# Perceiver block, context projection: values laid out in memory by chunk, partition and head, last chunk's values computed sooner, its writes waited for in the next stage

## What is computed

```python
q = (x @ Wq).reshape(B, N, HEADS, hd).transpose(0, 2, 1, 3)
k = (context @ Wk).reshape(B, M, HEADS, hd).transpose(0, 2, 1, 3)
v = (context @ Wv).reshape(B, M, HEADS, hd).transpose(0, 2, 1, 3)
scores = jnp.einsum('bhid,bhjd->bhij', q, k) * scale
scores = jnp.where(context_mask[:, None, None, :], scores, max_neg)
attn = jax.nn.softmax(scores, axis=-1)
```

## Time and profile before

| | us |
|---|---|
| median of three runs | 3372.61 |
| the profiled execution | 3372.62 |
| its span in the trace | 3370.9 |
| PE busy | 2945.2 (87%) |
| DVE busy | 1830.0 (54%) |
| ACT busy | 1350.9 (40%) |
| POOL busy | 404.1 (12%) |

### The profile page before, as it was taken

One profiled execution on the slowest core, in us unless ns is written; L12 is line 12 of the kernel. 1 busy time (PEld: TensorE's weight loads), 2 busy tenths in 40 slices (PEclk: granted clock), 3 DMA queues, 4 the chain that ended last, 5 costly groups with the idle time before them and its releaser, 6 DMA issues. The chain is left out here.

```text
span 3370.9 us, 66496 instructions
## 1 busy us (share of the span) xinstructions
PE 2945.2 (87%) x27158; PEld 2487.7 (74%) x27158; DVE 1830.0 (54%) x3246; ACT 1350.9 (40%) x2191; POOL 404.1 (12%) x571
## 2 busy tenths in 40 slices
PE   6999809998768999477999669999999999999978
PEld 6888706776564777463777455999999999999867
DVE  5555418774527775446776343555555555555524
ACT  4444305665003666123667120444444444444311
POOL 2443400000100000000000002220202020200000
PEclk9999958998787999686999685999999999999969
DMA  4898879882468883158884271100101010000016
GB/s 154 281 289 270 269 152 182 177 176 64 153 187 177 174 176 78 46 191 178 175 176 101 82 220 36 52 18 22 39 1 39 1 39 1 1 1 1 17 50 227
DMA packets 251093, 393.95 MB, mean 117 GB/s; under 512 B 45827, under 2 KB 214149, under 8 KB 250789
## 3 DMA queue, kind: packets, MB, share of 16 engines
q1 hardware_dynamic: 250791, 389.70, 45.3%
HBM read 289.45 MB, written 99.49 MB: 115 GB/s over the span
## 5 line engine op out<-in xcount | busy, mean ns | idle before, releaser
L712 DVE TENSOR_REDUCE L_xattn_tops<-psum 128x1 f32<-128x896 f32 x672 | 702.4, 1086 | 270.3 <-PE psum L564 269.1
L625 ACT ACTIVATE L_xattn_probs<-psum 128x512 f32<-128x512 f32 x1176 | 612.3, 600 | 518.2 <-PE psum L575 518.1
L1720 DVE TENSOR_TENSOR L_units_low<-psum,L_units_high 128x896 fp32r<-128x896 f32 x224 | 243.6, 1088 | 486.8 <-ACT L_units_high L1669 486.8
L564 PE MATMUL psum<-L_xattn_keys,L_xattn_q_stack 96*128 96x448 bf16 (+1 forms) x1344 | 395.2, 378 | 110.5 <-DMA L_xattn_q_stack<-query_parts 65.2
L1637 PE MATMUL psum<-wide_tokens,L_units_high 128*128 128x386 f32 x1568 | 456.5, 358 | 1.4 <-DVE L_units_low L1720 1.4
L575 PEld LDWEIGHTS psum<-L_xattn_q_stack,L_xattn_keys 99*128 99x128 bf16 (+1 forms) x4704 | 323.1, 98 | 144.4 <-issue 19.2
L575 PE MATMUL psum<-L_xattn_q_stack,L_xattn_keys 99*128 99x128 bf16 (+1 forms) x4704 | 394.2, 221 | 5.0 <-ACT L_xattn_probs L625 5.0
L1638 PE MATMUL psum<-wide_tokens,L_units_low 128*128 128x194 f32 x1568 | 395.1, 252 | 0.0
L588 PE MATMUL psum<-L_xattn_probs,L_xattn_values 128*17 128x128 f32 x9408 | 358.5, 277 | 0.2 <-issue 0.2
L1669 ACT CAST L_units_high<-psum 128x896 fp32r<-128x896 f32 x224 | 203.3, 908 | 363.7 <-PE psum L1625 363.7
L1661 ACT ACTIVATE L_units_raw<-L_units_raw,L_units_negmax 128x896 f32<-128x896 f32 x224 | 221.6, 1036 | 308.4 <-DVE L_units_negmax L1711 308.4
(11 more groups left out here) (436 smaller groups left out, 3990.6 us busy)
## 6 DMA issues: line engine op xcount, KB each, us to landing
key_parts<-proj_parts SPq DMA_DIRECT2D x84, 672.0 KB, 5.1
L_xattn_keys<-key_parts SPq DMA_DIRECT2D x144, 336.0 KB, 4.7
values_scratch<-proj_values SPq DMA_DIRECT2D x18, 1904.0 KB, 11.9
L_xattn_values<-values_scratch SPq DMA_DIRECT2D x144, 238.0 KB, 5.4
L_ffn_w<-in_L_ffn_W SPq DMA_DIRECT2D x32, 1024.0 KB, 6.8
L_xattn_keys<-key_parts SPq DMA_DIRECT2D x144, 224.0 KB, 5.0
L_xattn_keys<-key_parts SPq DMA_DIRECT2D x192, 112.0 KB, 5.1
L_ffn_w<-in_L_ffn_w SPq DMA_DIRECT2D x16, 1024.0 KB, 6.3
```

The lines of the kernel that those rows point to most:

```text
L564: last = pe.matmul(top_slot(n)[:, s, :], q_stack[0:P1, h, :], keys[0:P1, v % RING, key:key + WIN // 2], start=True, stop=True)
L625: act.activation(group_probs(k), score_bank(k), ACT.Exp).then_inc(sem("probs"), 1)
L712: dve.tensor_reduce(tops[:, h % 2, 2 * c + w:2 * c + w + 1], top_slot(n), AX.XY, ALU.max)\
L1720: dve.tensor_tensor(low[gr][:], turned_banks(gr), high[gr][:], ALU.subtract).then_inc(sem("low"), 1)
```

## The change

- **Layout.** `g.values` is (layer, chunk, partition, head, 14 x 17) instead of (layer, head, chunk, partition, 14 x 17). A write of a layer's chunk is 128 runs of 15232 bytes. A load of one head's values still reads runs of 952 bytes, now 15232 bytes apart instead of one behind the other.
- **Last two halves.** Their order is written out as `LAST`: 12 key tiles, with two value tiles behind each of the first seven. PE waits for both halves' `split` ahead of it. The last chunk goes out in three whole writes at key tiles 7, 8 and 9 of the twelve, the chunk before it at tiles 0, 2 and 4.
- **Waits.** The projection no longer waits for its writes. Their semaphores outlive the stage; the next one's SP waits for them after the load of the query weights and ahead of the rows of ones. There `keys`, `values` and `probs` are allocated last.
- **Beginning.** SP loads context half 0 first, then the six `w_a` tiles, half 1, and writes the mask row. ACT issues the mask's load, the twelve `w_b` loads and the four biases. Half 0 is rounded and split ahead of the weights.
- **Mask.** The work on the mask (DVE, one matmul, the write of the row) is moved from layer 0's cross-attention to the projection's beginning.

```diff
+        late = [("value", i, t) for i in (NH - 2, NH - 1) for t in range(GT)]
+        LAST = []
+        for i in (NH - 2, NH - 1):
+            for n in range(NK2):
+                LAST.append(("key", i, n))
+                LAST.extend(late[:2])
+                del late[:2]
...
             def store_values(c, l):
                 sp.wait_ge(sem("values"), TPC * (c + 1))
-                dst = dram(g.values, l * g.layer_values + c * 128 * TPC * VW,
-                           [[TPC * VW, 128], [NCH * 128 * TPC * VW, H], [1, TPC * VW]])
-                src = values[c % 2][:, l * H:l * H + H, :, :].rearrange("p h t e -> p h (t e)")
-                sp.dma_start(dst, src).then_inc(sem(f"values_out{c % 2}"), 16)
...
+                dst = dram(g.values, l * g.layer_values + c * 128 * H * TPC * VW,
+                           [[H * TPC * VW, 128], [1, H * TPC * VW]])
+                src = values[c % 2][:, l * H:l * H + H, :, :].rearrange("p h t e -> p (h t e)")
+                sp.dma_start(dst, src).then_inc(written(f"values_out{c % 2}"), 16)
...
+            load(0)
             for l in range(NL):
                 cols = slice(l * D, l * D + D)
                 for w, name in ((0, "Wk"), (1, "Wv")):
...
+                    sp.dma_start(w_a[:, w, cols], a[f"L{l}_xattn_{name}"][0:128, :]).then_inc(sem("weights"), 16)
             load(1)
-            for i in range(NH):
+            sp.wait_ge(sem("drop"), 1)
+            sp.dma_start(dram(g.mask_row, 0, [[NK // 128, 128], [1, NK // 128]]), drop_bf[:])\
+              .then_inc(written("mask_out"), 16)
+            for i in range(NH - 2):
                 for n in range(NK2):
...
-            for l in range(NL):
-                store_last(1, l)
-            for r in range(RING):
-                sp.wait_ge(sem(f"parts_out{r}"), 16 * len(range(r, NH * NK2, RING)))
-            for r in range(2):
-                sp.wait_ge(sem(f"values_out{r}"), 16 * NL * (len(range(r, NCH, 2)) + (r == (NCH - 1) % 2)))
+            for n in range(2 * NK2):
+                store_parts((NH - 2) * NK2 + n)
+                if n in (0, 2, 4):
+                    store_values(NCH - 2, n // 2)
+                if n in (7, 8, 9):
+                    store_values(NCH - 1, n - 7)
...
+            pe.wait_ge(sem("some"), 1)
+            pe.matmul(bank(g, 7, 0, 1), g.ones[:], some[:], start=True, stop=True).then_inc(sem("mask_count"), 1)
             pe.wait_ge(sem("weight_parts"), 4)
-            for i in range(NH):
+            pe.wait_ge(sem("drop"), 1)
+            for i in range(NH - 2):
...
+            pe.wait_ge(sem("split"), 2 * NH)
+            for kind, i, n in LAST:
+                (key_tile if kind == "key" else value_tile)(i, n)
...
+            act.dma_start(mask8[:], a["mask"].rearrange("(p n) -> p n", p=128)).then_inc(sem("mask"), 16)
+            for l in range(NL):
...
+                        act.dma_start(w_b[copy * C1:copy * C1 + C1, w, cols], a[f"L{l}_xattn_{name}"][128:C, :])\
+                           .then_inc(sem("weights"), 16)
...
+            round_context(0)
             act.wait_ge(sem("weights"), LOADS)
             act.copy(wh_a[:], w_a[:]).then_inc(sem("weights_rounded"), 1)
             act.copy(wh_b[:], w_b[:]).then_inc(sem("weights_rounded"), 1)
-            round_context(0)
             round_context(1)
```

In `streamed_cross_attention`, SP's part:

```diff
-                    src = dram(g.values, layer * g.layer_values + (h * NCH + c) * 128 * TPC * VW,
-                               [[TPC * VW, 128], [128 * TPC * VW, n], [1, TPC * VW]])
+                    src = dram(g.values, layer * g.layer_values + (c * 128 * H + h) * TPC * VW,
+                               [[H * TPC * VW, 128], [128 * H * TPC * VW, n], [1, TPC * VW]])
...
                 if masked:
-                    sp.dma_start(mask8[:], a["mask"].rearrange("(p n) -> p n", p=128)).then_inc(sem("mask"), 16)
+                    for r in range(PARTS_RING):
+                        sp.wait_ge(g.drain.sem(f"parts_out{r}"), 16 * 2 * NCH)
+                    for r in range(2):
+                        sp.wait_ge(g.drain.sem(f"values_out{r}"), 16 * 3 * len(range(r, NCH, 2)))
+                    sp.wait_ge(g.drain.sem("mask_out"), 16)
...
                 if masked:
-                    sp.wait_ge(sem("drop"), 1)
-                    sp.dma_start(dram(g.mask_row, 0, [[NK // 128, 128], [1, NK // 128]]), drop_bf[:])\
-                      .then_inc(sem("mask"), 16)
-                    sp.wait_ge(sem("mask"), 32)
```

More of the change, by code:

```diff
@@ L74, in block, with adopt @@
         return self.ctx.enter_context(self.nc.Block())
+    def adopt(self, other):
+        self.sems.update({f"{other.tag}_{name}": sem for name, sem in other.sems.items()})
     def clear(self):
@@ L196, in project_context @@
     ND = NL * D
-    RING = 6
+    RING = PARTS_RING
     with ExitStack() as ctx:
         st = Stage(nc, ctx, "proj")
-        sem = st.sem
+        sem, written = st.sem, g.drain.sem
+        mask8, maskf = st.sb("mask8", [128, NK // 128], U8), st.sb("maskf", [128, NK // 128])
+        some = st.sb("some", [128, 1])
+        drop, drop_bf = st.sb("drop", [128, NK // 128]), st.sb("drop_bf", [128, NK // 128], BF16)
         raw_a = [st.sb(f"raw_a{i}", [128, W]) for i in range(2)]
@@ L337, in round_context @@
                    .then_inc(sem("rounded"), 1)
+            act.dma_start(mask8[:], a["mask"].rearrange("(p n) -> p n", p=128)).then_inc(sem("mask"), 16)
+            for l in range(NL):
+                cols = slice(l * D, l * D + D)
+                for w, name in ((0, "Wk"), (1, "Wv")):
+                    for copy in range(2):
+                        act.dma_start(w_b[copy * C1:copy * C1 + C1, w, cols], a[f"L{l}_xattn_{name}"][128:C, :])\
+                           .then_inc(sem("weights"), 16)
+                if l > 0:
+                    for k in range(DG):
+                        act.dma_start(bk[:, l, k:k + 1], dram(a[f"L{l}_xattn_bk"], 128 * k, [[1, 128], [1, 1]]))\
+                           .then_inc(sem("weights"), 16)
+            round_context(0)
             act.wait_ge(sem("weights"), LOADS)
@@ L356, in _ @@
         def _(dve):
+            link = chain(dve, sem("dve_step"))
             dve.memset(bk[:, 0, :], 0.0).then_inc(sem("bk_zero"), 1)
@@ L400, in _ @@
                 take_value(i, GT - 1)
-                if i + 2 < NH:
-                    low_context(i + 2)
+                low_context(i + 2)
+            for kind, i, n in LAST:
+                (key_rest if kind == "key" else take_value)(i, n)
             dve.tensor_reduce(g.ctx_sum[:], sums[:], AX.X, ALU.add)
@@ L447, in stage @@
             sem = st.sem
+            if masked:
+                st.adopt(g.drain)
             wq, bq = st.sb("wq", [128, DG, D]), st.sb("bq", [128, DG])
@@ L548, in _ @@
                 last.then_inc(sem("q_in_psum"), 1)
-                if masked:
-                    pe.wait_ge(sem("some"), 1)
-                    pe.matmul(bank(g, 2, 0, 1), g.ones[:], some[:], start=True, stop=True)\
-                      .then_inc(sem("mask_count"), 1)
                 pe.wait_ge(sem("stack"), STACK)
@@ L2812, in build @@
         g.clip = sb("clip", [1, 1], I32)
+        g.any_key = sb("any_key", [128, 1])
+        g.drain = Stage(nc, ctx, "written")
         g.ctx_sum = sb("ctx_sum", [128, 2])
```

69 lines of the change are left out of this document (25 added, 44 removed).

## The result

The kernel after takes 3318.71 us (median of four runs, 3315.55 to 3320.49), the kernel before beside it 3372.97 (four runs): a ratio of 0.9831, 95% interval 0.9814 to 0.9848, 54 us less. The forecast was 3316. The profiled execution of after took 3317.55 us, its span is 3315.8.

A forecast was written before the change was run, and what follows sets the result against it. PE's work with gaps from waits for value writes, then a 48.8 us write drain, bounded the changed stretch. Terms gave -53.2 us to the rows of ones and -3.1 in the opening: 3372.6 - 56.3 = 3316, range 3303 to 3347.

The forecast's parts named there:

- four marks: Forecast times: PE's first matmul 22.6, its last projection matmul 382.5, rows of ones issued 405.9, first scores 444.6 us.
- Part 1: Projection's beginning: 17 DMA issues on ACT at 0.57 us each; PE starts at 22.6 instead of 27.25, -4.6 us.
- the last landed 1.6 us behind its issue: Projection's beginning: the last weight load lands at 15.1 us, so ACT can round the weights from 16.8.
- Part 2: Values layout: long writes at 369 GB/s; four DVE waits of 4.2 us; PE's loss falls from 32.7 to 3.2, -29.5 us.
- the method of the 266 GB/s: Window 150 to 200: full-engine time less other traffic at 369 GB/s leaves 22.0 us for 5.85 MB of values.
- Part 3: Last two halves: PE's 4.4 us stop before half 12 costs +6.0, keys alone +1.3; PE ends at 382.5.
- Part 4: Drain behind the projection: last chunk's writes from 378.6, 9.3 MB at 369 GB/s; ones at 405.9, -53.2 us altogether.
- Part 5: Next stage's opening, ones to first scores: the 8.1 us mask wait goes, but only -3.1; 38.7 us stay.
- That time was the queue's: Opening: head 0's loads were still landing during the mask wait, so query parts land behind them: -3.1, not -8.1 us.
- Case B: Rival, chance 0.25: long value writes no faster than 952-byte runs; four waits stay, drain grows by 6.1; 3345 us.
- Case C: Rival, chance 0.11: nothing waits, as long runs beat 369 GB/s or the queue is emptier; 3308 us.
- Case D: Rival, chance 0.04: scattered value reads slow three layers' streams; kernel slower, 3412 us if reads take 2.2 times as long.

## Why the prediction was right

The forecast came true within 3 us, its four marks within 1.7. The mechanism was right: the long runs move values at about the key writes' rate, and the waits and the drain shrink with it. That the number is as close as 3 us is partly luck, since the time behind layer 0 alone scatters by up to 12 us between profiles and misses of 1 to 2 us cancel below. By its parts:

- **Part 1.** Forecast -4.6, measured -3.1. The step that was off is "the last landed 1.6 us behind its issue": it was 4.8, with half 1's context in the queues. The issues on ACT (0.61 each, forecast 0.57), the table load behind them and the hidden mask chain (its last operation ends at 9.65) were right.
- **Part 2.** Right in mechanism, a little short in size. DVE's wait 13.4 us, longest 4.2, against 4 x 4.2; PE lost 0.8 us once, not four times. The context loads of 61.95 and 311.60 are ten halves apart, 249.65 us for 248.6. So about 1 us stays of the 32.7, forecast 3.2. By the method of the 266 GB/s, the window 150 to 200 of after gives 0.85 x 50 = 42.5 us of full engines for 15.7 MB; less 9.85 MB at 369 (26.7) leaves 15.8 for 5.85 MB: 370, the value taken. The two layout kernels give the same pair: 266 again in after with the old layout (305 GB/s at 0.95), 377 with the layout alone (320 at 0.86). All four are estimates that take 369 for the rest of the traffic.
- **Part 3.** The stop of 4.44 was forecast at 4.4, and PE's end came at 382.4 for 382.5, but in that end misses cancel: PE started 1.6 late and lost 2.2 less in the waits; another 0.5 I can't place. The order cost PE 7.4, forecast 7.3: by the differences above 5.5 for the stop with what it covers (forecast 6.0) and 1.8 for the keys alone (1.3). I set no price against it for what the order saves in the drain, and it saves nothing: 21.8 us from PE's end to the ones, 20.4 in the old order.
- **Part 4.** Key 7's third part at 378.76 (378.6). The drain took 25.0 us and not 27.3: the engines gave 389 GB/s and not 369, which makes 1.3 us on 9.3 MB, and 1.0 I can't place. Less the 0.6 us by which it began late (379.21 for 378.6), that is the 1.7 us at the ones. The sum doesn't say which part of the drain's gain the half-chunk writes are; by the old-order kernel it is some 15 us.
- **Part 5.** Forecast 38.7, measured 39.9; the writes of the query parts landed behind head 0's loads (12.0 us to the next issue, 5.1 in the earlier trace rows). The mask row's wait, forecast at 3.1, is worth 2.0 between before and after and 2.6 to 4.0 by the kernel with the mask back. "That time was the queue's" was right, but 12.4 of the 39.9 us pass behind the rows of ones, which I had in a row and didn't ask about.

So the 56.8 us at the first scores are, step by step: 35.8 for the layout; 32.0 from there to the old order with everything else of after, of which 25.4 lie between PE's end and the ones, 3.6 before PE's end and 2.9 in the opening; and 10.9 lost again by the new order of the last two halves.

Case B, no faster than 952 bytes, is refuted by the two layout kernels. The rule that spoke for it was the Trainium skill's (DMA: Bandwidth & Descriptors, Specifications), 512 bytes for line rate: here runs of 952 bytes went at 266 and of 15232 bytes at 370 GB/s of full engines, so the measurement decides against it, with the reserve that distance and length of the runs changed together. Case C would have needed no wait and a drain at more than 369: waits are nearly gone and the drain was faster, yet the opening kept its 39.9. Case D is refuted by the windows: in after, PE is busy 220.00 of 220 us from 503 to 723 at a DMA share of 0.85, as in the earlier trace rows; layers 1 and 2 take 372.3 and 364.4 us in the table above, 371.7 and 364.4 before; a head's values, in pieces 15232 bytes apart, land in 5.1 us (median, 5.2 before).

From the first scores on, 2871.7 us are left in after and 2870.0 before. The 56.8 us that the trace shows at the first scores are 60.1 at `out_wo` and 55.1 in the span; the difference is within the scatter between profiles behind that mark.

## What to carry to other kernels

Lay out what is written under a bound in the longest runs, and let the reader, who has slack, take the short ones; look at GB/s by share of the engines, not at the share, to see which writes pay. When the last tiles' order is changed to shorten a drain, set what PE's end moves against what the drain moves: here 7 to 10 us were paid for nothing. An earlier first product in a streamed stage is worth only what the stream of loads behind it gains as well, so read the mark at the stage's end. Before a small difference between two traces is put down to an edit, look whether it is there already ahead of the first instruction that the edit changed, as 1.2 and 1.4 us were here.

## What the runs showed of the hardware

By estimate, runs of 952 bytes to memory went at 266 GB/s of full engines, runs of 15232 at 370 to 377. Key parts (runs of 1792 bytes) alone and with long values moved 369 to 418 GB/s by share (214 at 0.58; 426 at 1.02). Runs of 476 bytes were the slowest: 952 KB landed in 17.0 to 18.2 us, far apart or close. A DMA into three partitions with runs of 256 bytes went at 19 GB/s with 0.16 of the engines, and what SP issued behind it took 12.4 us to issue for 1.8; with runs of 3584 bytes 7.5. DMA issues on ACT cost 0.61 us each, SP's beside them 0.33 to 0.61.
